# Grouped attention and a displacement layer on one core: the softmax sums of the sixth head pair, the order of the projection and of the x statistics, and weight preparation in half units

## The reference, cut to what matters

```python
# x: (8, 768, 32, 32); 12 heads of 64 channels, N = 1024 positions
q, k, v = split(tokens(group_norm(x)) @ W_qkv.T)        # q is not used further
scores  = var(v, over 64 channels) outer var(k, over 64 channels) * 64**-0.5
out     = softmax(scores) @ v                           # per head, 1024 x 1024
x = x + from_tokens(out @ W_proj.T + b_proj)            # layer 0
x = x + displace(group_norm(x))                         # layer 1: shift each channel, 3x3 depthwise taps
```

## Time and profile before

| | |
|---|---|
| time, median of 3 runs | 2051.96 us (2048.73 to 2055.91) |
| profiled execution, its own time | 2052.81 us |
| its span | 2051.1 us |
| PE busy | 1977.6 us, 96% |
| DVE busy | 1721.8 us, 84% |
| ACT busy | 1207.1 us, 59% |
| granted TensorE clock, mean | 0.994 |

### The profile page before, as it was taken

The page is one execution under the profiler, slowest core; times in us unless marked ns, Lnnn a source line. Parts: engine busy times, 40 slices in busy tenths (PEclk is TensorE's granted clock), DMA queues, the critical chain, the costliest instruction groups (busy, mean ns, idle before and its releaser), DMA issues.

```text
span 2051.1 us, 33578 instructions
## 1 busy us (share of the span) xinstructions
PE 1977.6 (96%) x12736; PEld 1113.4 (54%) x12736; DVE 1721.8 (84%) x3647; ACT 1207.1 (59%) x1322; POOL 271.0 (13%) x324
## 2 busy tenths in 40 slices
PE   5899999999999999999999999999999999999997
PEld 4656437553566536664375634756356553755443
DVE  7598777998689977899869997899868997589967
ACT  3466734677357762777627773477636777177820
POOL 2000001121011110111001210111101211011121
PEclk9999999999999999999999999999999999999998
DMA  8211312446234452445524472254523454144515
GB/s 327 83 53 48 118 65 74 135 145 176 83 113 156 127 166 70 130 132 171 159 63 125 136 196 92 82 146 136 166 83 125 145 163 117 44 129 119 155 42 184
DMA packets 110193, 255.19 MB, mean 124 GB/s; under 512 B 47312, under 2 KB 48080, under 8 KB 110032
## 3 DMA queue, kind: packets, MB, share of 16 engines
q0 software_dynamic: 31968, 116.41, 19.8%
q1 hardware_dynamic: 72016, 114.62, 18.1%
q10 hardware_dynamic: 6048, 22.02, 3.2%
HBM read 172.93 MB, written 79.73 MB: 123 GB/s over the span
## 4 chain that ended last, share of the span: by engine, by line
PE 69%; DVE 15%; DMA 6%; issue 5%; ACT 4%; SPq 1%; ACTq 0%; POOL 0%; DVEq 0%; POOLq 0%
PE ps L1397 28%; PE ps L1439 20%; PE ps L1454 17%; DVE bt L938 5%; DVE st L890 3%; ACT ring L712 3%; DMA a_sb<-a_rows 3%; PE ps L1414 2%; DMA a_rows<-at 2%; DMA xv<-in_L_conv_W_qkv 1%; DVE bt L1061 1%; DVE bt L1058 1%; DMA dt_sb<-d_sb 1%; DVE xv L1071 1%; DVE xv L1074 1%
## 5 line engine op out<-in xcount | busy, mean ns | idle before, releaser
L712 ACT ACTIVATE ring<-a_sb,coef 128x1024 f32<-128x1024 f32 x768 | 817.9, 1137 | 30.6 <-DMA a_sb<-a_rows 13.5
L1397 PE MATMUL ps<-wkv_hi,h_sp 128*128 128x256 f16 x4608 | 773.2, 274 | 11.0 <-DVE wkv_lo L1253 10.7
L1439 PE MATMUL ps<-ring,xv 128*64 128x512 f32 x3072 | 690.0, 598 | 15.8 <-ACT ring L712 14.4
L1397 PE MATMUL ps<-wkv_lo,h_sp 128*128 128x256 f16 x2304 | 630.0, 273 | 0.0
L938 DVE TENSOR_TENSOR bt<-bt,ring 128x1024 f32<-128x1024 f32 x512 | 597.0, 1213 | 2.9 <-ACT ring L712 1.7
L1397 PEld LDWEIGHTS ps<-wkv_hi,h_sp 128*128 128x128 f16 x4608 | 452.3, 98 | 91.7 <-issue 26.8
L1439 PEld LDWEIGHTS ps<-ring,xv 128*64 128x64 f32 x3072 | 210.0, 137 | 433.8 <-issue 392.8
L696 ACT ACTIVATE xv<-ps 128x256 f32<-128x256 f32 x192 | 72.5, 382 | 574.5 <-DVE st L890 573.6
L1454 PE MATMUL ps<-xv,wp_hi 128*128 128x512 f16 x1152 | 349.0, 379 | 3.2 <-DVE xv L1180 1.8
L890 DVE BATCH_NORM_STATS2 st<-ps 128x6 f32<-128x64 f32 x1536 | 217.2, 211 | 97.9 <-PE ps L1397 97.1
L1397 PEld LDWEIGHTS ps<-wkv_lo,h_sp 128*128 128x128 f16 x2304 | 226.1, 98 | 27.3
(11 more groups left out here) (174 smaller groups left out, 1362.9 us busy)
## 6 DMA issues: line engine op xcount, KB each, us to landing
a_sb<-a_rows SPq DMA_DIRECT2D x96, 512.0 KB, 4.9
out<-xv POOLq DMA_DIRECT2D x84, 512.0 KB, 5.3
xv<-in_x POOLq DMA_DIRECT2D x48, 512.0 KB, 3.6
h_sp<-in_x ACTq DMA_DIRECT2D x42, 512.0 KB, 5.5
shift_rows<-bt POOLq DMA_DIRECT2D x42, 512.0 KB, 3.3
bt<-r_rows SPq DMA_DIRECT2D x80, 256.0 KB, 4.1
bt<-in_x SPq DMA_DIRECT2D x24, 512.0 KB, 9.8
shift_rows<-ring SPq DMA_DIRECT2D x12, 528.0 KB, 15.4
```

What stands on the lines that cost most here:

```text
L712: nc.scalar.activation(ring_of(p, s, m), a_sb[:, h % 4, :], ACT.Exp, scale=coef[:, h, m:m + 1]).then_inc(s_exp, 1)
L1397: last = nc.tensor.matmul(ps[:, kv_bank[u % 2], half * 2 * P:(half + 1) * 2 * P], h_sp[:, k, hp, m * P:(m + 1) * P], wkv[wpart][:, k, q * ...
L1439: last = nc.tensor.matmul(ps[s * HD:(s + 1) * HD, o_bank[p % 2] + j, :], v_sb[:, p, m, s * HD:(s + 1) * HD], ring_of(p, s, m)[:, j * HALF: ...
```

## The change

1. `MD[5]` goes from 7 to 8: the eighth key tile of the sixth pair is also added on DVE, and four matmuls per image go.
2. The projection of unit 4 over pairs 0 to 3 stands ahead of the closing `denominators` of pair 5, that of unit 5 right behind `r_spread`. The pair-5 output is evicted to `g_t` in place of `r_t`, without a wait for `o_second` of pair 4, and `r_spread` writes the bank that this output has left. All six units then take pair 4, and then pair 5.
3. The statistics of image b+2 move out of phase A into `group_end`, beside projection units 6 to 10. This holds for images 0 to 5, image 0 included. Their aggregation stands in phase A, the small DMAs on them behind pair 1 in place of pair 4. Of the loads, only the last tile now waits for the taps.
4. `a_transpose(5)` stands inside `weigh(4, 1)`, two matmuls ahead of its old place.
5. In phase A of image 0, the weight units follow each half of a k/v unit: three per half (two per half in the last two k/v units) in place of six or five per unit. ACT does them ahead of `v_evict`.

```diff
-        MD = (7, 8, 8, 8, 6, 7)
+        MD = (7, 8, 8, 8, 6, 8)
...
-        W_SIDE = (6, 6, 5, 5, 5, 5)
+        W_SIDE = (3, 3, 3, 3, 3, 3, 3, 3, 2, 2, 2, 2)
...
-                    if p == 4 and later and with_next:
+                    if p == 1 and later and with_next:
                         stats_to_groups(sp, "x", b)
...
             def o_evict_last(b):
                 act.wait_ge(s_pv, (b + 1) * (NT // 2))
-                act.wait_ge(s_olo, b * NP + NP - 1)
...
             def phase_a(b, beside=None):
                 for u in range(UA):
+                    if beside is not None:
+                        beside(2 * u)
+                        beside(2 * u + 1)
                     v_evict(b, u)
-                    if beside is not None:
-                        beside(u)
...
-                    if staged and u <= 2:
-                        staged_stats(b + 1, u)
...
-                    if staged and u >= UQ:
-                        staged_stats(b + 1, u - 1)
+                    if staged and u == UQ:
+                        channel_aggregate("x", b + 1)
...
+            STAGED_AT = {6: (0,), 7: (1, 2), 8: (3,), 9: (4,), 10: (5,)}
...
                         channel_stats("y", (u - 1) // 2, (u - 1) % 2, x1)
+                    if staged and u in STAGED_AT:
+                        for n in STAGED_AT[u]:
+                            staged_stats(b + 2, n)
...
             def body(b, with_next):
-                group_end(b, True)
+                group_end(b, True, with_next)
...
+                    if j == 0 and amid is not None:
+                        a_transpose(b, amid)
...
-                    if u == UQ:
+                    if u == UQ or beside is not None:
                         kv_unit(b, u, later, (0,))
-                        a_transpose(b, 0)
+                        if beside is not None:
+                            beside(2 * u)
+                        if u == UQ:
+                            a_transpose(b, 0)
                         kv_unit(b, u, later, (1,))
+                        if beside is not None:
+                            beside(2 * u + 1)
...
+                    if p == NP - 1:
+                        pe.wait_ge(s_at, b * NP + NP)
+                        project(b, 4, range(CT - 2))
                     pe.wait_ge(s_acc, b * NADD + ADDS_TO[p + 1])
...
                 r_spread(b)
+                project(b, 5, range(CT - 2))
                 pe.wait_ge(s_olo, b * NP + NP - 1)
-                for u in range(4):
+                for u in range(6):
                     project(b, u, [CT - 2])
-                pe.wait_ge(s_on, b * NP + NP)
-                for u in (4, 5):
-                    project(b, u, range(CT - 1))
```

More of the change, by code:

```diff
@@ L112, in gn_attention_displace @@
         y_t = [ring[:, t, :] for t in range(CT)]
-        x_st = [ring[:, 6, :], ring[:, 7, :], t_t] + [acc[:, i, :] for i in range(3)]
+        x_st = [ring[:, 6, :], ring[:, 7, :]] + [acc[:, i, :] for i in range(3)] + [t_t]
         tail_g = [ring[:, t, :] for t in range(CT)]
@@ L1085, in phase_a @@
                             group_spread_y(dve, l1)
-                    if staged and u <= 2:
-                        staged_stats(b + 1, u)
-                    if beside is not None:
-                        beside(u)
+                    if beside is not None and u != UQ - 1:
+                        beside(2 * u + 1)
                     if u == UQ - 1:
                         variances(b, 0)
+                        if beside is not None:
+                            beside(2 * u + 1)
                         a_out(b, 0, l1 is not None)
@@ L1115, in span @@
                         if (p, m) == (NP - 1, 4):
-                            for n in range(4, MT - 1):
+                            for n in range(4, MT):
                                 add_up(b, p, n, later)
@@ L1423, in d_bank_free, with weigh @@
                     pe.wait_ge(s_rlast, b)
-            def weigh(b, p, m, later):
+            def weigh(b, p, m, later, amid=None):
                 if m == 0:
@@ L1477, in span @@
                             kv_unit(b, nxt + m // 2 + 1, later)
-                        weigh(b, p, m, later)
-                        if p <= 4 and m == (3 if p <= 3 else 1):
+                        weigh(b, p, m, later, p + 1 if (p, m) == (4, 1) else None)
+                        if p <= 3 and m == 3:
                             a_transpose(b, p + 1)
@@ L1496, in r_spread @@
                         row = 32 * (2 * s + j)
-                        last = nc.tensor.matmul(ps[s * HD:(s + 1) * HD, D_BANK + j, :], ones[row:row + 1, 0:HD],
+                        last = nc.tensor.matmul(ps[s * HD:(s + 1) * HD, o_bank[(NP - 1) % 2] + j, :], ones[row:row + 1, 0:HD],
                                                 d_sb[row:row + 1, :], start=True, stop=True)
```

47 lines of the change are left out of this document (25 added, 22 removed).

## The result

| | before | the change |
|---|---|---|
| time, median | 2053.93 us (2048.73 to 2055.92, 4 runs) | 2027.41 us (2025.74 to 2028.36, 4 runs) |
| ratio to before, 95% interval | | 0.9881 (0.9855 to 0.9907) |
| span of the profiled execution | 2051.1 us | 2026.0 us |
| granted clock, mean | 0.994 | 0.997 |

The kernel is 24.4 us faster by the ratio and 25.1 us by the two spans, where 15.2 were forecast. The direction was right and the size was not.

A forecast was written before the change was run, and what follows sets the result against it. TensorE's own work was taken to bound seven of eight images, with waits in phase A and at the end of image 0. −13.9 − 6.2 + 4.5 + 0.4 = −15.2 gave 2036.8 us; 8 in 10 within 2030 to 2045.

The forecast's parts named there:

- Part 1: Phase A of image 0: weight units behind each half k/v unit cut TensorE's waits, phase 39.7 us, −13.9 taken.
- Part 2: Pair 5, eighth tile added on DVE: four matmuls fewer, no new wait, 0.89 us in each of seven images, −6.2.
- Part 3: x statistics beside the last projection units: free in middle images; end of image 0 +4.5, including 1.8 from late closing sums.
- Part 4: Earlier transpose of the sixth pair's variances: 0, but +0.4 in the last image; moved small DMAs of x statistics: 0.
- Better than the sum: Rival: earlier transpose brings exponentials forward (−5), or the 3.3 us pause shrinks and its restart goes (−3); 2030 us, chance 15%.

## Why the prediction was wrong, by its own steps

**Part 1** was right: −13.9 forecast, 14.0 in the trace, 14.2 alone. There are two waits of 1.04 us each, each right behind one of the two reductions for which VectorE was reckoned one us short, and no restart.

**Part 2** was right in the middle images. The closing sums wait for nothing, and from the start of pair 5 to the next image the change takes 64.73 us in five of six, for 65.48 to 66.00: 0.75 and more, for 0.89. With the 1.8 us at the end of image 0 that the prediction booked under part 3, it forecast −6.2 + 1.8 = −4.4, and 4.3 were measured alone. That these meet so closely is in part luck, since two terms were off, in opposite directions. At the end of image 0 items 1 and 2 cost 4.1 us and not 1.8: from the start of pair 5 to the first k/v matmul of image 1 it is 67.6 us before and 71.8 with them alone, by the wait of 4.97 and the half clock behind it. And in image 7 a wait for the closing sums of an early pair, which the prediction didn't look at, is 1.4 to 1.5 us in the traces of five of the six kernels without items 1 and 2, and at most 0.4 in all with them. Before and after, all such waits:

```profile
PE ps L1414 <- DVE bt L938: 1.7, 2, 1.5
```

```profile
PE ps L1422 <- DVE bt L940: 0.5, 1, 0.5
```

**Part 3** was right in its sum at the end of image 0: +4.5 forecast, 4.95 in the trace. Its shares (1.8 for the late closing sums, 2.7 for the statistics) don't stand side by side as it reckoned. Alone, the first costs 4.1 there, and the second 2.65 us of wait and some 1.7 for the half clock behind it. Together they cost 4.95, since TensorE's slow stretch and VectorE's longer list pass in the same time; that a restart falls there the prediction did say. Taking only the statistics away gives back 1.0 in the trace, not 2.7. The middle images show no wait for the statistics, as forecast. But the run with item 3 alone was 6.0 us faster, 3.1 more than the small DMAs alone, where the statistics were to cost 2.7; this difference is not explained.

**Part 4** is the part that failed, and not in its transpose. That gave 0.8 alone and 1.8 in the change, neither clear of nothing, and `a_rows` still lands with the broadcast ahead of it (at 950.02 us in image 3, behind 949.73). The step that failed is its last one, on the moved small DMAs of the x statistics: "Only DVE waited for those: 0". It asked who waits for these DMAs, and not whom they make wait. The first of them stood right behind the broadcast on which pair 5's exponentials depend, as 768 packets, and that broadcast landed 1.1 us later for it. Measured: 2.9 us alone (1.0 to 4.7), and 6.8 us given up when that one line is put back in the change. By the Trainium skill, page DMA: Bandwidth & Descriptors, section Issuing engines are not separate DMA queues, DMAs of all issuers interleave on the same sixteen engines. The traces agree: pair 5's broadcast takes 7.05 us with the small DMA behind it and 5.89 where only the small DMAs are moved, and pair 2's, behind which it then stands, 6.40 for 5.40. So a DMA without a reader near it is not free if one with a reader is under way.

Added up, the items alone give 14.2 + 4.3 + 6.0 + 0.8 = 25.3 us, and the change 24.4 to 25.2. The sums agree, the single items less so: left out of the change they are worth 12.4 (item 5), 6.2 (items 1 and 2), 6.3 to 6.8 (the small DMAs, for 2.9 alone) and 1.3 (the transpose), each with an uncertainty of 2 us or more. Against the forecast's −13.9, −4.4, +2.7 and +0.4, the miss of 10 us is 8.7 on part 3 with its DMAs and 1.2 on the transpose. Of the 8.7 the small DMAs are shown to be 2.9 to 6.8. The remaining 2 to 6 are not pinned to a step, and may in part be noise of the measurement, 1 to 2 us for each ratio. Of the 5.2 us of excess in image 7, 1.5 are the wait named under part 2, and up to 3.0 are chance: from the start of pair 5 of image 7 on, TensorE is at half the clock for 17.1 us in all before and for 11.1 after, but for 16.6 and 14.3 in the two repeats of the change. The rival "Better than the sum" had the right place, the exponentials of pair 5 and the pause of 3.3 us, and a half-right account, that all DMAs shift; the cause it named first, the transpose, was the wrong one, and at 2030 it was still 2.6 us above the result.

## What to carry to other kernels

Price a moved DMA twice: by who waits for it, and by which transfers it shares the engines with at its old and at its new place. Here 6.0 KB in 768 packets went with a delay of some 1 us of a broadcast of two times 512 KB; that the number of packets did it, and not the bytes, is not shown, since no run changed one without the other. Here the moved DMA delayed the broadcast at its new place as much, so such a DMA belongs behind a transfer with room. And ask of a row of waits for exponentials not only which engine is named in it, but which broadcast that engine waited for, and what was issued right behind that broadcast. Where a change has several parts, each alone and each left out tell whether they add up: here the total did, within the noise, and the largest miss that was found lay in a part that was called free. And look behind a sum that comes out right: in part 2 it did with two terms off.

## What the runs showed of the hardware that was not expected

A DMA of 6.0 KB in 768 packets, issued 0.5 us behind a broadcast of two times 512 KB, goes with a later landing of that broadcast: 7.05 us with it and 5.89 without at pair 5, 6.40 with it and 5.40 without at pair 2. Its own landing hardly differs, 7.6 us behind pair 4 and 7.1 behind pair 1 (medians). The DMA that reads the 6.0 KB back took 6.0 us behind pair 4 and 1.8 behind pair 1. Since it is issued only when the broadcast has landed, it is not the broadcast that slows it; what does was not looked into.

A wait of 4.52 us of TensorE was followed by a granted clock of 0.50 from 276.2 to 279.6 us, half of 2.4 GHz, and one of 2.99 us by 0.51 over as long; the two waits of 1.04 us in phase A were followed by none.

The granted clock reads 1.00 also where it was not recorded. TensorE's first k/v matmuls, behind 10.7 us of waiting, start every 0.21 us, and those of the next half unit every 0.11. The first row is of the change, whose record of the clock begins at 44.1 us; the second is the same place in the change without items 1 and 2, whose record begins at 25.1:

```profile
39.00:41.00 2.00, 2.00 (x10) 1.41 (x11) 0.21 (x2) 0.00 (x0) 0.00 (x0) 1.00 1.02 412
```

```profile
39.22:41.22 2.00, 2.00 (x10) 1.44 (x11) 0.21 (x2) 0.00 (x0) 0.00 (x0) 0.50 1.02 412
```

So the first unit does run at the 1.2 GHz level, as the prediction said, and a 1.00 at the start of a trace is to be held against the distance between matmuls.
